# Decoder layer on one core: other instruction orders in the slots, an earlier rope table, unread TensorE products, and the last quads summed by TensorE

## The chip, the cores and the metric

The kernel runs on one core of one Trainium2 chip. The metric is the device time of one execution in microseconds; what is compared is the median over several runs. A profile shows one execution, with times from the start of its span. The engines are TensorE (PE), VectorE (DVE), ScalarE (ACT), GpSimd (POOL), and SyncE (SP), which only starts transfers.

## The reference

One decoder layer over 32 sequences of 128 tokens with 128 features, all in float32:

```python
x = layernorm(x + self_attention(x))        # 16 heads of 64, rope on 32 of the 64, causal
x = layernorm(x + cross_attention(x, ctx))  # 16 query heads of 8, 4 key/value heads, rope, key mask
x = layernorm(x + moe(x))                   # 8 experts, top 2 of sinkhorn gates (3 rounds)
# moe(x) itself returns x + expert output, so the last sum holds 2*x
# expert: (relu(x @ wg) * (x @ wp)) @ wo, 256 hidden
```

## The kernel before

**The attention phase** (attention_phase, L92 on) is a software pipeline written out by hand. There are 36 slots, 0 to 35. In slot s five stages run, each for another sequence: f (q and k projection and rope) for sequence s, v (values) for s-1, k (self attention, output projection) for s-2, a (first norm, cross attention up to its scores) for s-3, c (cross attention from its probabilities on, second norm, router logits) for s-4. A q/k projection serves two sequences at once: even slots make the queries of a pair, odd slots the keys. So slots 0 to 3 fill the pipe, slots 4 to 31 are full, and slots 32 to 35 drain it (f is off in 32, v in 33, k in 34, a in 35). The program has no loops at run time.

**The order.** Each engine executes its own list in order. The list of a slot is the function `slot` in the block of that engine: before, one branch for `s < DRAIN_SLOT` (32) and one for the rest. Between engines there are semaphores. The products of TensorE land in seven PSUM banks, and the dictionary of SlotRing says which product uses which bank; a bank is reused in program order, so a product waits until its bank's last content was taken out (drained). Names like `k.S0` are a stage and a product: `k.S` scores, `k.PT` transposed probabilities, `k.OT` head outputs, `k.Y` the output projection; `a.T`, `a.QKV`, `a.QT`, `a.KT`, `a.S` and `c.PT`, `c.OT`, `c.O`, `c.T`, `c.Y`, `c.XT`, `c.R` are the steps of cross attention and router in their order; `f.XT`, `f.Q` and `v.V` are the transposed input, the projections and the values. Each is taken out by DVE or ACT, and which of the two does it is fixed by the list in which its `copy` stands (L649 on DVE, L486 on ACT).

**Steps that the prediction speaks of.** Rope: ACT copies a projection to `raw` (L520), POOL multiplies by the sine (L401), DVE by the cosine (rope_cos, L699); the sum is made by POOL (L410), in slots 0 and 1 by DVE (L707). Softmax: DVE takes the row maximum (L687), ACT the exponential with its sum (L505), DVE the reciprocal (L692), POOL multiplies (L395). cross_rope (L757 to L764) empties bank 0 of `a.QKV`; `f.Q2` uses bank 0 too. The second norm writes `x_all` (L723), reading SBUF alone.

**The start.** SP loads a third of the projection weights, the identity, the first inputs, then sixteen small tables, the rope tables as the seventh and eighth. In slot 0 DVE calls make_constants after x_lo: it waits for all small tables, copies the rope tables to a padded tile (L667), TensorE transposes them (turn_tables, last of its list in slot 0), DVE takes them out as cosT and sinT (L669 to L671), splits the second third of the weights (w_split(1), L655) and makes masks (L673 to L679). The rope steps need cosT and sinT. POOL splits the last third (L390) ahead of its first rope step.

**Routing.** The 32 sequences are routed in two groups, of 20 and 12. The steps of group 0 are laid at marks a, b, c, d of slots 24 to 31 (MARKS); its rows are then sent to their places in DRAM by 40 indirect transfers of POOL in slots 32 to 35 (send_rows, L1591).

**The FFN phase** (ffn_phase) works through 78 blocks of 128 gathered rows, 47 and 31; block i: transpose (L1907), three products for the hidden layer (L1914 to L1916), two transposes (L1922), two products (L1929), and POOL sends the answers (L1760). The routing steps of group 1 are laid beside blocks 0 to 23 (ROUTED), then POOL sends its 24 pieces. At the end eight quads of four sequences are joined: add the two answers (L1856), add 2x (L1861), statistics (L1867, L1872), deviation and normalise on ACT (L1788, L1796), and a store. Quads 5, 6 and 7 belong to group 1 and come last.

Of the kernel before, what the change touches and what calls it, by code (L numbers as in the profile page):

```python
# [6 lines left out]
F32 = mybir.dt.float32  # L7
# [4 lines left out]
ALU = mybir.AluOpType  # L12
# [10 lines left out]
COLS = 512  # L23
# [10 lines left out]
class SlotRing:  # L34
# [5 lines left out]
    def __init__(self, sem, banks, last):  # L40
        self.orders = [list(banks), list(last)]
# [7 lines left out]
    def count(self, s, name, back=0):  # L49

        total = 0
        for slot in range(s - back + 1):
            mates = [other for other in self.orders[slot >= DRAIN_SLOT] if self.banks[other] == self.banks[name]]
# [6 lines left out]
EVEN = ("f.XT0", "f.XT1")  # L60

# [58 lines left out]
def attention_phase(nc, sem, ps, x2_all, logits, ident, mhalf, eps, scratch, x, ctx, qmask, kpad, cosq, sinq,  # L120
# [5 lines left out]
    with ExitStack() as phase:  # L126
        def sb(name, shape, dt=F32):
# [104 lines left out]
        ident_loaded = sem("ident_loaded")  # L232
        wqkv_loaded = [sem(f"wqkv_loaded{third}") for third in range(3)]
# [38 lines left out]
                 (xwo_sb[:], xwo), (rw_sb[:], rw), (rb_sb[:], rb), (cos_sb[:], cosq), (sin_sb[:], sinq),  # L272
# [95 lines left out]
        def _(pool):  # L368
# [62 lines left out]
            def slot(s, r, f, v_, k, a, c):  # L431
                p = r % 2
                if s < DRAIN_SLOT:
# [7 lines left out]
                    if on(f):  # L441
                        rope_add(s, r, 0)
                    if on(k):
                        norm_fill(k, 2)
# [1561 lines left out]
```

## Time and profile before

| | |
|---|---|
| median of 3 runs | 991.24 us (989.80 to 991.57) |
| the profiled execution, its own time | 994.09 us |
| its span | 992.3 us |
| granted TensorE clock, mean of the span | 0.92 |
| busy | PE 834.2, DVE 694.7, ACT 673.9, POOL 647.7 us |

The page of the profile gives busy time by engine and 40 slices of the span. Other views cut it into stretches, group instructions by line and shape, list who waited for whom, or list instructions in order of time. A full slot is the stretch from one `k.S` product group (L1000) to the next.

### The profile page before, as it was taken

The numbers are of one execution on the slowest core, as the hardware profiler recorded it, in microseconds if no ns is written. First come the engines' busy times: TensorE is split into PE (matmuls) and PEld (weight loads), VectorE is DVE, ScalarE is ACT, GpSimd is POOL, SyncE is SP. The second block draws the span as 40 slices with busy tenths as digits, with TensorE's granted clock in tenths as the row PEclk, the third lists the DMA queues.
The fourth block names the chain that finished last, engine by engine and source line by source line (L and its number), as shares of the span: only waits on it lengthen the run. The fifth ranks groups of instructions, "written<-read, shape, count | busy, mean of one in ns | idle before, by whom it ended". The sixth has DMA issues, their size and how long they took to land. (4 is left out here: it accounts for less than half of the span.)

```text
span 992.3 us, 22962 instructions
## 1 busy us (share of the span) xinstructions
PE 834.2 (84%) x7560; PEld 662.6 (67%) x7592; DVE 694.7 (70%) x1885; ACT 673.9 (68%) x2427; POOL 647.7 (65%) x706
## 2 busy tenths in 40 slices
PE   3689999999999999999988988897766698179990
PEld 2577787877878777788867776775543476157760
DVE  4647878888788887888888888885455466035674
ACT  3358878888788887888887787785464353035564
POOL 4477867878678786787876667677656145745551
PEclk7789999999999999999999999998885599579995
DMA  4000409900000000000000000000101511141334
GB/s 126 6 7 12 125 23 131 103 12 7 15 8 15 13 7 16 7 13 14 8 15 7 12 7 13 6 7 18 35 24 44 133 36 36 52 117 45 111 89 127
DMA packets 63506, 39.81 MB, mean 40 GB/s; under 512 B 15936, under 2 KB 60224, under 8 KB 63392
## 3 DMA queue, kind: packets, MB, share of 16 engines
q1 hardware_dynamic: 58848, 28.89, 13.4%
q0 software_dynamic: 4544, 9.45, 2.9%
q8 instruction: 65, 1.06, 0.5%
q14 instruction: 49, 0.40, 0.1%
HBM read 21.51 MB, written 16.81 MB: 39 GB/s over the span
## 5 line engine op out<-in xcount | busy, mean ns | idle before, releaser
L401 POOL TENSOR_TENSOR crossed<-raw,sinT 128x512 f32<-128x512 f32 x128 | 162.9, 1283 | 162.5 <-ACT raw L520 156.5
L505 ACT ACTIVATE prob<-ps,negmax 128x128 f32<-128x128 f32 x512 | 181.3, 383 | 81.1 <-DVE negmax L687 81.1
L395 POOL TENSOR_TENSOR prob<-prob,recip 128x512 f32<-128x512 f32 x128 | 133.0, 1048 | 12.0 <-DVE recip L692 11.8
L513 ACT ACTIVATE xprob<-ps,xmax 128x128 f32<-128x128 f32 x512 | 136.0, 416 | 7.0 <-DVE xmax L687 6.8
L1760 POOL DMA_INDIRECT answered<-ysb,goes_to x78 | 76.2, 977 | 91.8 <-DVE ysb L1851 58.9
L687 DVE TENSOR_REDUCE negmax<-ps 128x4 f32<-128x512 f32 x128 | 84.2, 679 | 43.7 <-PE ps L1000 30.9
L505 ACT ACTIVATION_READ_ACCUMULATOR prob<-ps,negmax 128x1 f32 x512 | 114.2, 223 | 0.0
L934 PE MATMUL ps<-ident,xprob 128*128 128x128 f32 x514 | 83.5, 288 | 18.8 <-ACT xprob L513 8.1
L972 PE MATMUL ps<-xT_hi,w_lo 128*128 128x256 f32 x256 | 82.6, 323 | 13.5 <-DVE xv L764 6.3
L687 DVE TENSOR_REDUCE xmax<-ps 128x4 f32<-128x512 f32 x128 | 82.2, 684 | 16.6 <-remote 9.5
L520 ACT ACTIVATE raw<-ps 128x512 f32<-128x512 f32 x128 | 80.5, 629 | 16.8 <-POOL crossed L401 10.3
L934 PEld LDWEIGHTS ps<-ident,xprob 128*128 128x128 f32 x514 | 61.6, 146 | 29.3 <-DVE xprobT L649 10.3
L410 POOL TENSOR_TENSOR kR<-kR,crossed 128x512 f32<-128x512 f32 x60 | 76.2, 1280 | 4.1 <-DVE kR L699 2.9
L934 PE MATMUL ps<-ident,prob 128*128 128x128 f32 x512 | 73.6, 278 | 6.2 <-POOL prob L395 4.7
L410 POOL TENSOR_TENSOR qR<-qR,crossed 128x512 f32<-128x512 f32 x60 | 76.1, 1280 | 1.2
L1591 POOL DMA_INDIRECT placed<-x_all,place x64 | 63.3, 988 | 18.3 <-issue 18.3
L973 PE MATMUL ps<-xT_lo,w_hi 128*128 128x256 f32 x256 | 74.1, 290 | 0.0
L974 PE MATMUL ps<-xT_hi,w_hi 128*128 128x256 f32 x256 | 74.1, 289 | 0.0
L1000 PE MATMUL ps<-kR,qR 32*128 32x128 f32 x2048 | 70.3, 285 | 0.5 <-DVE kR L707 0.4
L1019 PE MATMUL ps<-probT,v 128*64 128x128 f32 x1024 | 69.8, 279 | 0.5 <-issue 0.5
L1000 PEld LDWEIGHTS ps<-kR,qR 32*128 32x128 f32 x2048 | 63.5, 194 | 7.2 <-issue 6.2
L1845 DVE TENSOR_TENSOR h<-ps,gs 128x256 f32<-128x256 f32 x78 | 33.1, 424 | 50.0 <-ACT gs L1779 27.3
(221 smaller groups left out, 2246.3 us busy)
## 6 DMA issues: line engine op xcount, KB each, us to landing
xg<-placed SPq DMA_DIRECT2D x8, 528.0 KB, 6.6
yq<-answered SPq DMA_DIRECT2D x8, 512.0 KB
placed<-fw_hi SPq DMA_DIRECT2D x1, 3008.0 KB, 17.4
xf<-in_x SPq DMA_DIRECT2D x32, 64.0 KB, 2.9
xres<-in_x SPq DMA_DIRECT2D x32, 64.0 KB, 1.8
cx<-in_ctx SPq DMA_DIRECT2D x32, 64.0 KB, 1.8
out_y<-yo SPq DMA_DIRECT2D x8, 256.0 KB, 2.3
placed<-fw_hi SPq DMA_DIRECT2D x1, 1984.0 KB, 25.4
```

The source lines that it names most:

```text
L395: nc.gpsimd.tensor_tensor(prob[:, n], prob[:, n], recip[:, n, :, None].broadcast_to([128, 4, S]), ALU.mult).then_inc(normed, 1)
L401: nc.gpsimd.tensor_tensor(crossed[n % 2][:], raw[n % 2][:, ::-1], sinT[:, :, None, :].broadcast_to([128, 2, 2, S]), ALU.mult).then_inc(sin ...
L410: nc.gpsimd.tensor_tensor(dst, dst, crossed[n % 2][:], ALU.add).then_inc(roped, 1)
L505: last = nc.scalar.activation(prob[:, n, j, :], bank(name)[:, j * S:(j + 1) * S], ACT.Exp, bias=negmax[:, n, j:j + 1], accum_out=sums[:, n ...
L513: last = nc.scalar.activation(xprob[:, n, g, :], bank(name)[:, g * S:(g + 1) * S], ACT.Exp, bias=xmax[:, n, g:g + 1])
L520: nc.scalar.activation(raw[n % 2][:].rearrange("p a b s -> p (a b s)"), bank(f"f.Q{n}"), ACT.Copy).then_inc(raw_ready, 1)
L687: nc.vector.tensor_reduce(dst, bank(name).rearrange("p (j s) -> p j s", j=4), AX_X, ALU.max, negate=True).then_inc(done, 1)
L934: return nc.tensor.transpose(dst, src, ident[:])
L972: nc.tensor.matmul(part, w_lo[:, at:at + S], hi[:], start=True, stop=False)
L973: nc.tensor.matmul(part, w_hi[:, at:at + S], lo[:], start=False, stop=False)
L1000: last = nc.tensor.matmul(bank(f"k.S{n}")[:, g * S:(g + 1) * S], qR[pair][rows, g, ab, p, :], kR[rows, g, ab, p, :], start=False, stop=(g ...
L1760: nc.gpsimd.indirect_dma_start(answered[g], bass.IndirectOffsetOnAxis(goes_to[g][:, j:j + 1], 0), ysb[:, i, :], None, bounds_check=plan.si ...
```

## The change

What it does, part by part:

- **Full slots.** Other lists for all four engines in slots 0, 1 and 4 to 31, and another bank for most products. On DVE the copies of `c.PT1`, `c.OT`, `v.V1` and `c.XT` are new, on ACT those of `c.PT2` and `k.PT0`.
- **Slots 2 and 3** get lists of their own (FILL_SLOTS).
- **Slots 32 to 35** get other lists.
- **Slot 0.** The rope tables are loaded right after the first third of the weights and are turned right after the first input. w_split(1) moves behind the second rope step, the masks to the end of slot 1, POOL's split of the last third to the end of slot 0.
- **Unread products.** `busy(s, n)` issues n products of 128x512 in bf16 into the free bank 7 in slots 34 and 35, where nothing reads them: 27 in slot 34, 22 in slot 35, 8 behind slot 35, 3 of 128x128 in float32 at the first block of the FFN phase, 8 of 128x512 in float32 behind its last block.
- **Last quads.** For quads 6 and 7 TensorE makes the sum in PSUM: twice the identity times x, plus the identity times each of the two answers. DVE takes the statistics from PSUM. The second half of quad 7 is normalised by DVE, the first by ACT, and the shift and normalise of a quad of group 1 now stand ahead of the moments of the next.

The diff, cut to its core:

```diff
+FILL_SLOTS = (2, 3)
...
         ring = SlotRing(sem, {
...
-            "a.T": 1, "c.PT3": 2, "a.QKV": 0, "c.OT": 2, "v.V0": 1, "c.O": 2, "k.PT0": 4, "v.V1": 5, "c.T": 1, "k.PT1": 2,
-            "f.Q1": 3, "c.Y": 6, "f.Q2": 0, "f.Q3": 1, "k.PT2": 2, "k.PT3": 4, "k.OT0": 3, "a.QT": 5, "a.KT": 6, "k.OT1": 4,
+            "a.T": 1, "f.Q0": 6, "c.OT": 0, "v.V0": 1, "c.O": 0, "a.QKV": 6, "f.Q1": 5, "c.T": 1, "v.V1": 2, "k.PT0": 1,
+            "c.Y": 0, "k.PT1": 4, "f.Q2": 6, "k.PT2": 3, "k.OT0": 1, "k.PT3": 2, "f.Q3": 4, "a.QT": 3, "a.KT": 0, "k.OT1": 2,
...
             sp.dma_start(stage[0], third(wqkv, 0)).then_inc(wqkv_loaded[0], 16)
+            sp.dma_start(cos_sb[:], cosq).then_inc(rope_loaded, 16)
+            sp.dma_start(sin_sb[:], sinq).then_inc(rope_loaded, 16)
             sp.dma_start(ident[:], ident_d).then_inc(ident_loaded, 16)
...
-            pool.wait_ge(w_hi_ready, 3)
-            nc.gpsimd.tensor_tensor(third(w_lo, 2), stage[2], third(w_hi, 2).bitcast(F32), ALU.subtract).then_inc(w_lo_ready[2], 1)
             pool.wait_ge(tables_made, 1)
+            def w_split():
+                pool.wait_ge(w_hi_ready, 3)
+                nc.gpsimd.tensor_tensor(third(w_lo, 2), stage[2], third(w_hi, 2).bitcast(F32), ALU.subtract).then_inc(w_lo_ready[2], 1)
...
+            dve.wait_ge(rope_loaded, 32)
+            dve.wait_ge(pads_set, 2)
+            for i, table in enumerate((cos_sb[:, 0:ROPE // 2], sin_sb[:, ROPE // 2:ROPE])):
+                nc.vector.tensor_copy(turning[i][:, :, 0, :], table[:, None, :].broadcast_to([128, 4, ROPE // 2])).then_inc(pads_made, 1)
             w_split(0)
...
+                        if s == 0:
+                            make_tables()
...
+                        if s == 0:
+                            w_split(1)
...
+                        if s == 1:
+                            make_constants()
...
-                if isinstance(s, int) and s == 1:
-
+                if s == 2:
                     pe.wait_ge(w_loaded, 16 * len(small))
                     pe.wait_ge(masks_made, 1)
                     pe.wait_ge(const_ready, 4)
 
+                def busy(s, n):
+
+                    if s < B + 2:
+                        return
+                    for _ in range(n):
+                        nc.tensor.matmul(ps[:, 7, :], identb[:], causal[:].rearrange("p j s -> p (j s)"), start=True, stop=True)
...
             slots(pe, slot)
+            for _ in range(8):
+                nc.tensor.matmul(ps[:, 7, :], identb[:], causal[:].rearrange("p j s -> p (j s)"), start=True, stop=True)
...
+        SUMMED = {left[-2]: [5], left[-1]: [6, 7]}
         for q in left:
-            late_steps += [(name, q) for name in ("add", "twice", "stats", "moments", "deviation")]
+            if q not in SUMMED:
+                late_steps += [("add", q), ("twice", q)]
+            late_steps.append(("stats", q))
+            if q > left[0] and plan.quads[q - 1][0]:
+                late_steps += [("shift", q - 1), ("normalise", q - 1)]
+            late_steps += [("moments", q), ("deviation", q)]
...
+            nc.vector.tensor_scalar(twin[:], ident[:], 2.0, None, ALU.mult).then_inc(twin_made, 1)
...
                         x_transpose(0)
+                        for _ in range(3):
+                            nc.tensor.matmul(ps[:, DOWN, 0:128], ident[:], ident[:], start=True, stop=True)
...
+            for q in SUMMED:
+                b0 = plan.quads[q][1]
+                sums(q, twin, x2_all[:, b0:b0 + FB, 0:D], True, False)
+
+            for _ in range(8):
+                nc.tensor.matmul(ps[:, UP[0], :], ident[:], x2_all[:, 0:FB, 0:D], start=True, stop=True)
+            for q in SUMMED:
+                pe.wait_ge(yq_loaded[q % QB], 16 * (quads_before(q % QB, q) + 1))
+                sums(q, ident, yq[q % QB][:, :, 0:D], False, False)
+                sums(q, ident, yq[q % QB][:, :, D:2 * D], False, True).then_inc(quad_summed, 1)
```

How instructions move, at three places.

DVE at the start, from its first instruction to the first rope step of slot 0, before (`w_lo` is w_split, `qR<-ps,cosT` the first rope step):

```order
L655 SCALAR_TENSOR_TENSOR w_lo<-prob,w_hi 128x4x128 x2
L727 TENSOR_TENSOR xT_lo<-ps,xT_hi 128x256
L667 COPY xprob<-cos_sb 128x4x16
L667 COPY xprob<-sin_sb 128x4x16
L669 COPY cosT<-ps 128x128
L670 TENSOR_SCALAR sinT<-ps 128x128
L671 COPY sinT<-ps 128x128
L655 SCALAR_TENSOR_TENSOR w_lo<-prob,w_hi 128x4x128 x2
L673 CAST qm_all<-qm_u 128x32
...
L1406 RECIPROCAL rtemp<-rtemp 128x1
L699 TENSOR_TENSOR qR<-ps,cosT 128x512
```

and with the change:

```order
L741 COPY xprob<-cos_sb 128x4x16
L741 COPY xprob<-sin_sb 128x4x16
L732 SCALAR_TENSOR_TENSOR w_lo<-prob,w_hi 128x4x128 x2
L806 TENSOR_TENSOR xT_lo<-ps,xT_hi 128x256
L746 COPY cosT<-ps 128x128
L747 TENSOR_SCALAR sinT<-ps 128x128
L748 COPY sinT<-ps 128x128
L778 TENSOR_TENSOR qR<-ps,cosT 128x512
```

The second w_split and the masks left the way to the first rope step; w_split(1) now stands behind the second rope step, the masks behind the last one of slot 1.

DVE in slot 24, the middle of the slot, before (`la<-dif,rlog` is a routing step, `xt` and `xv` are cross_rope, `xo` is `c.O` divided):

```order
L743 TENSOR_TENSOR xo<-ps,xrec 128x128
L692 RECIPROCAL recip<-sums 128x4
L649 COPY probT<-ps 128x512
L1444 TENSOR_TENSOR la<-dif,rlog 128x160
L757 TENSOR_TENSOR xt<-ps,xcos_sb 128x160
L762 TENSOR_TENSOR xt<-ps,xsin_sb 128x20x4 x2
L764 COPY xv<-ps 128x4x8
```

and with the change:

```order
L822 TENSOR_TENSOR xo<-ps,xrec 128x128
L771 RECIPROCAL recip<-sums 128x4
L766 TENSOR_REDUCE negmax<-ps 128x4
L771 RECIPROCAL recip<-sums 128x4
L836 TENSOR_TENSOR xt<-ps,xcos_sb 128x160
L841 TENSOR_TENSOR xt<-ps,xsin_sb 128x20x4 x2
L843 COPY xv<-ps 128x4x8
L1669 TENSOR_TENSOR la<-dif,rlog 128x160
L726 COPY v<-ps 128x512
```

cross_rope now stands ahead of the routing step, and a copy of values stands where one of probabilities stood earlier.

TensorE in slot 35, before (`xprob` are the four `c.PT`, then `c.OT`, `c.O`, `c.T`, `c.Y`, `c.XT`, `c.R`):

```order
L934 MATMUL ps<-ident,xprob 128x128 x16
L1074 MATMUL ps<-xprobT,xv 32x512 x4
L934 MATMUL ps<-ident,xoT 128x128 x4
L934 MATMUL ps<-ident,xo 128x128
L1091 MATMUL ps<-xwo_sb,xonT 128x128
L934 MATMUL ps<-ident,x_all 128x128
L1099 MATMUL ps<-rw_sb,x2T 128x8
```

and the same stretch with the change, from the last `c.PT` on (`causal,identb` at L1247 and L1463 are unread products):

```order
L1070 MATMUL ps<-ident,xprob 128x128 x4
L1247 MATMUL ps<-causal,identb 128x512 x3
L1210 MATMUL ps<-xprobT,xv 32x512 x4
L1247 MATMUL ps<-causal,identb 128x512 x2
L1070 MATMUL ps<-ident,xoT 128x128 x4
...
L1227 MATMUL ps<-xwo_sb,xonT 128x128
L1247 MATMUL ps<-causal,identb 128x512 x6
L1070 MATMUL ps<-ident,x_all 128x128
...
L1235 MATMUL ps<-rw_sb,x2T 128x8
L1463 MATMUL ps<-causal,identb 128x512 x8
```

The read products are the same and keep their order; unread ones stand between them.

## Rows read from the trace of the kernel before

**Rows 1.** The page: busy time by engine, its share of the span and instructions.

```profile
PE 834.2 (84%) x7560; PEld 662.6 (67%) x7592; DVE 694.7 (70%) x1885; ACT 673.9 (68%) x2427; POOL 647.7 (65%) x706
```

**Rows 2.** Stretches of the span: length, busy time of PE, PEld, DVE, ACT, POOL, clock.

```profile
38.10:59.50 21.40, 17.19 (x165) 15.07 (x166) 8.10 (x18) 11.44 (x43) 13.84 (x12) 0.76 0.03 9
59.50:82.30 22.80, 19.66 (x187) 16.84 (x187) 13.31 (x34) 16.58 (x62) 16.30 (x18) 0.85 0.03 9
82.30:499.20 416.90, 403.31 (x4221) 328.48 (x4240) 339.64 (x853) 353.98 (x1312) 317.34 (x340) 1.00 0.18 31
499.20:681.80 182.60, 164.67 (x1704) 133.10 (x1710) 154.61 (x399) 146.00 (x545) 128.48 (x136) 1.00 0.03 9
681.80:713.50 31.70, 22.00 (x191) 15.62 (x191) 14.02 (x39) 15.90 (x62) 18.33 (x22) 0.80 0.10 31
713.50:741.00 27.50, 19.22 (x178) 14.39 (x177) 11.98 (x34) 13.29 (x54) 17.51 (x20) 0.86 0.10 31
741.00:777.40 36.40, 20.88 (x79) 12.33 (x79) 18.53 (x48) 14.06 (x39) 19.68 (x23) 0.55 0.12 36
```

**Rows 3.** Instructions in order of time, 9 to 21 us: start, length, what.

```profile
9.37 0.60 ACT L520 ACTIVATE raw<-ps 128x512 f32<-128x512 f32 x1 [2.27 <-PE ps L974]
...
13.55 0.89 DVE L667 COPY xprob<-cos_sb 128x64 f32<-128x64 f32 x1 [5.91 <-DMA eidx_sb<-in_eidx]
...
15.91 2.35 DVE L655 SCALAR_TENSOR_TENSOR w_lo<-prob,w_hi 128x512 fp32r<-128x512 f32 x2
...
20.53 0.69 DVE L699 TENSOR_TENSOR qR<-ps,cosT 128x512 f32<-128x512 f32 x1
```

**Rows 4.** Groups by line and shape in slots 13 and 14: DVE and ACT copies.

```profile
L649 DVE COPY v<-ps 128x512 f32<-128x512 f32 x2 | 1.4, 692 | 0.6 <-PE ps L986 0.6
...
L486 ACT ACTIVATE x2T<-ps 128x128 f32<-128x128 f32 x2 | 0.6, 283 | 0.0
```

**Rows 5.** Waits in 501 to 685 us: total, times, longest.

```profile
PEld ps L972 <- DVE xv L764: 7.3, 5, 2.4
```

**Rows 6.** Waits in 640 to 777 us.

```profile
DVE negmax L687 <- remote: 12.9, 2, 6.5
...
DVE xmax L687 <- remote: 9.5, 2, 4.8
```

**Rows 7.** The costliest group of TensorE in 741 to 777 us.

```profile
L934 PE MATMUL ps<-ident,xprob 128*128 128x128 f32 x28 | 7.1, 424 | 7.1 <-ACT xprob L513 7.1
```

**Rows 8.** Three bf16 products of 128x512 in a row, at 59 and 712 us.

```profile
58.72 0.81 PE L989 MATMUL ps<-causal,identb 128*128 128x512 bf16 x3
...
712.08 1.46 PE L989 MATMUL ps<-causal,identb 128*128 128x512 bf16 x3 [3.60 <-DVE logits L749]
```

**Rows 9.** The end of the attention phase and the first product of FFN blocks 2, 3, 6 and 7.

```profile
775.76 0.17 DVE L749 TENSOR_TENSOR logits<-ps,rb_sb 128x8 f32<-128x8 f32 x1 [0.39 <-PE ps L1099]
777.38 7.62 SPq L1721 DMA_DIRECT2D xg<-placed  x6
...
784.42 0.79 PE L1914 MATMUL ps<-fw_hi,x_lo 128*128 x1
787.20 0.78 PE L1914 MATMUL ps<-fw_hi,x_lo 128*128 x1
...
796.12 0.49 PE L1914 MATMUL ps<-fw_hi,x_lo 128*128 x1
797.91 0.49 PE L1914 MATMUL ps<-fw_hi,x_lo 128*128 x1
```

**Rows 10.** The last quads: DVE and ACT in order of time.

```profile
977.76 0.69 DVE L1856 TENSOR_TENSOR acc<-yq 128x512 f32<-128x512 f32 x1 [4.06 <-DMA yq<-answered]
...
979.21 0.87 DVE L1867 BATCH_NORM_STATS2 st<-acc 128x6 f32<-128x128 f32 x4
...
986.29 3.17 ACT L1796 ACTIVATE yo<-acc,nmr,rstd 128x128 f32<-128x128 f32 x8
```

**Rows 11.** Line 723, all its instructions: count, shortest, median, longest in ns.

```profile
L723 DVE TENSOR_SCALAR x_all<-y,mv,rstd x32: 337/1286/1299, 95.0 to 773.8; 128x128 f32<-128x128 f32 x32
```

More of the change, by code:

```diff
@@ L34, with __init__ @@
 class SlotRing:
-    def __init__(self, sem, banks, last):
-        self.orders = [list(banks), list(last)]
+    def __init__(self, sem, banks, first, last):
+        self.orders = [list(banks), list(first), list(last)]
         self.banks = banks
@@ L52, in count @@
         for slot in range(s - back + 1):
-            mates = [other for other in self.orders[slot >= DRAIN_SLOT] if self.banks[other] == self.banks[name]]
+            mates = [other for other in self.orders[2 if slot >= DRAIN_SLOT else 1 if slot in FILL_SLOTS else 0] if self.banks[other] == self.banks[name]]
             for other in mates if slot < s - back else mates[:mates.index(name) + 1]:
@@ L870, in slot @@
                     if on(c):
-                        copy(s, "c.PT0", xprobT[:, 0].rearrange("p j s -> p (j s)"))
+                        copy(s, "c.PT1", xprobT[:, 1].rearrange("p j s -> p (j s)"))
+                    if on(a):
+                        normalise(a, y1, mv1, rstd1, x1c[1 - p][:], rstd1_ready, x1_ready)
                     if on(k):
@@ L1206, in slot @@
                         xo_back()
+                    for stage_ in marked("pe", s, "b"):
+                        routing.pe(pe, 0, stage_)
+                    if on(a):
+                        xqkv()
+                    if on(f):
+                        qk(1)
+                    if on(c):
+                        xo_transpose()
+                    if on(v_):
+                        values(1)
+                    if on(k):
+                        prob_transpose(0)
+                    if on(c):
+                        xout()
@@ new lines, in slot @@
+                    if on(k):
+                        prob_transpose(1)
+                    if on(f):
+                        qk(2)
+                    if on(k):
+                        prob_transpose(2)
+                        pv(0)
+                    for stage_ in marked("pe", s, "c"):
+                        routing.pe(pe, 0, stage_)
+                    if on(k):
+                        prob_transpose(3)
+                    if on(f):
+                        qk(3)
+                    if on(a):
+                        xqk_transpose()
@@ new lines, in slot @@
+                    if on(k):
+                        pv(1)
+                    if on(c):
+                        x2_transpose()
+                    if on(a):
+                        xscores(0)
+                        xscores(1)
+                        xscores(2)
+                    if on(c):
+                        router()
+                    if on(a):
+                        xscores(3)
+                    for stage_ in marked("pe", s, "d"):
+                        routing.pe(pe, 0, stage_)
@@ L1215, in slot @@
                         xout()
+                        busy(s, 6)
                     if on(k):
@@ L1877, in shift, with normalise @@
                     .then_inc(nmr3_ready, 1)
-            quad_steps = {"add": add, "twice": twice, "stats": stats, "moments": moments, "shift": shift}
+            def normalise(q):
+                if q < left[-1]:
+                    return
+                dve.wait_ge(nmr3_ready, q + 1)
+                wait(dve, stored[q % QB], 16 * quads_before(q % QB, q))
+                for j in range(FB // 2, FB):
+                    nc.vector.tensor_scalar(yo[q % QB][:, j, :], joined(q, j), rstd3[q % QB][:, j:j + 1], nmr3[q % QB][:, j:j + 1],
+                                            ALU.mult, ALU.add).then_inc(yo_ready, 1)
+            quad_steps = {"normalise": normalise, "add": add, "twice": twice, "stats": stats, "moments": moments, "shift": shift}
+            nc.vector.tensor_scalar(twin[:], ident[:], 2.0, None, ALU.mult).then_inc(twin_made, 1)
             split_x(0)
@@ L1953, in _, with sums @@
                     expert_down(i - 2, owners.pop(i - 2))
+            def sums(q, weights, src, start, stop):
+                each = FB // len(SUMMED[q])
+                for n, at in enumerate(SUMMED[q]):
+                    last = nc.tensor.matmul(ps[:, at, 0:each * D], weights[:], src[:, n * each:(n + 1) * each, :], start=start, stop=stop,
+                                            skip_group_check=True)
+                return last
+            pe.wait_ge(twin_made, 1)
+            for q in SUMMED:
[7 more added lines that the diff above has]
+                sums(q, ident, yq[q % QB][:, :, D:2 * D], False, True).then_inc(quad_summed, 1)
 def _tables():
```

461 lines of the change are left out of this document (310 added, 151 removed), and 14 rows, old and new, of the table ring.

## The prediction

> **What bounds the kernel now.** I read the page first: PE is busy 84% of the span, DVE 70, ACT 68, POOL 65 [rows 1]. A share over the whole span mixes stages, so I cut the span where a slot's first k.S product starts [rows 2]. Slots 4 to 23 take 416.9 us, 20.85 each, at the full clock (1.00 is 2.4 GHz), with PE busy 403.3: TensorE's list is the bound, and only 13.6 us, 0.68 per slot, are idle. Slots 24 to 31, which carry the routing steps, take 182.6 us, 22.8 each, with PE idle 17.9. The fill and the drain are chains of short steps over all engines: slots 2 and 3 take 21.4 and 22.8 us though two and one of their stages are missing, slots 32 and 33 take 31.7 and 27.5, and slots 34 and 35 with the barrier 36.4 at a mean clock of 0.55, so nearly all at 1.2 GHz. Behind that the FFN phase is paced by its blocks [rows 9], and the end by three quads in a row [rows 10].
>
> The profiled execution took 994.09 us, 1.8 more than its span and 2.85 above the median of 991.24. I sum against 994.09 and take 2.85 off at the end. A measurement of this kernel can tell about 0.2%, 2 us, from no change.
>
> **The start.** The first rope step begins at 20.53 us, though its input is copied by 9.97 (9.37 + 0.60) [rows 3]. DVE idles 5.91 us for the last small table, then turns tables, splits weights (2.35 from 15.91) and makes masks (18.26 to 20.53, 2.3). With the change the tables come early; I set the step at 11 us, a microsecond past the copy for the two loads now ahead of the input: 9.5 us off. 2.35 come back behind the second rope step and 2.3 before slot 2, whose first product waits for the masks; POOL's split, about as long, now stands before slot 1's rope steps. Left are 2.5 to 4.9 us. I take -3, and bounds of 0 (the rope chain was the bound, not its start) and -7.
>
> **Slots 2 and 3.** TensorE is idle 4.2 and 3.1 us there and runs partly at half clock [rows 2]. New lists can win at most those 7.3. The chain scores, exponential, normalisation, transposes, output projection stays; qk(0) moves ahead of the scores, qk(1) and both value products ahead of the first transpose, so less is left for the end. I take -3, bounds +2 and -7.
>
> **Full slots, 20 of them.** Work on TensorE is unchanged; a new order can only take idle time away, at most 0.68 a slot. DVE gains one large copy net (PT1, OT, V1 for PT2 and k.PT0, 0.69 us) and XT (I take ACT's 0.28) [rows 4], so 17.0 (339.6 / 20) becomes 18.0 of 20.85; ACT falls from 17.7 to 16.7. Nothing comes to its limit. I take -0.25 a slot, -5; bounds -13.6, and +5 if each slot loses as much.
>
> **Slots 24 to 31.** Against 20.85 a slot they cost 15.8 us extra. One wait has a name: qk(2) needs the bank that cross_rope empties, and cross_rope stands behind a routing step: 7.3 us [rows 5]. Now cross_rope stands ahead of it. Late next is DVE itself: 19.3 (154.6 / 8) plus 1.0 is 20.3 busy of 22.8. I take -6, bounds -15.8 and +5.
>
> **Slots 32 and 33.** 59.2 us with TensorE idle 18.0. Four times DVE waits long before a row maximum, 22.4 us in all, and the view names no engine (remote) [rows 6]. I can't say from the list alone what it waited for, so I don't count on that. Value products now stand before the scores and fill a gap. I take -3, bounds +4 and -10.
>
> **Slots 34 and 35.** TensorE's 20.9 busy us at clock 0.55 would be 11.5 at the full one, 9.4 less; TensorE waits for others half the time (a transpose group has as much idle before it, 7.1 us, as work [rows 7]), so half of that is on the path: -4.7. The price: three bf16 products take 0.81 us at full clock and 1.46 at half [rows 8], which makes 0.22 and 0.43 each. 49 are 10.8 us at full clock; they fit in the idle time, but a product that becomes ready behind them waits for those issued. Up to six stand in one place, where the wait is long; I take +1.3 for all. The eight behind slot 35 last 1.8 us where DVE's last step ends at 775.93 and SP goes on at 777.38 [rows 9]: about +1.3 to the barrier. Net -2, bounds +3 and -6.
>
> **FFN start.** The first products of blocks 2 and 3 are 2.78 us apart, those of blocks 6 and 7 1.79 [rows 9]. If the clock is up when the phase starts, three to four blocks win 0.99 each less some waiting: -3, bounds 0 and -4. The routing of group 1 is laid by blocks, so what is won here lasts through its dispatch.
>
> **The last quads.** From the first add to the last normalise it is 977.76 to 989.46 [rows 10]. Quads 6 and 7 lose add and twice, 1.4 us each on DVE (quad 5: 1.45 from add to statistics). In their place TensorE sums; a float32 product of 512 columns has no row. Four times the 0.25 us of rows 7 (7.1 for 28) is 1.0 at mostly half clock, 0.5 at full; two per quad, and twice that if each is two passes: 1 to 2 us a quad at full clock, up to 4 at half. At full clock the sums of quad 7 end some 1.5 us before the old place of its statistics. Behind the statistics stood deviation and eight normalise pieces (3.17); now four of them go ahead, and the last four are shared by two engines: 0.9 less. I take -2.4, bounds +1 and -4.
>
> **Sum:** -3 -3 -5 -6 -3 -2 -3 -2.4 = -27.4, so 966.7 profiled and **963.8 us** as a median, -2.8%. With each term near its size, 954 to 973.
>
> **Rivals.**
> A, *the full slots win nothing*: the idle 0.68 a slot is the cost of waits that any order has, and DVE's copy eats what routing slots win. Without -5 and -6: -16.4, 974.8 us. For it speaks that PE idle is so small already.
> B, *the full slots win more*: half of all PE idle goes there (-7) and most of the routing excess (-12): another -8 to -12, about 954 us.
> C, *the unread products do not hold the clock*. Against it: in the full slots, where PE is busy 97%, it stays at 1.00; for it: slots 32 and 33 are busy 70% and still are at 0.80 and 0.86 [rows 2]. Then 49 products are 21.1 us in 15.5 us of idle time, +5.6, the eight +3, nothing is won in the drain, the FFN start and the last quads: -3 -3 -5 -6 -3 +8.6 = -11.4, 979.8 us. The Trainium skill speaks for this rival (TensorE: Matmul & The Clock Gate, A second HAM failure mode): small idle times between groups of matmuls can make the clock go back and forth. By that rule, too, it is 979.8; the clock of 0.80 at 70% busy agrees with it.
> D, *slower: DVE becomes what a slot waits for*. DVE's waits (3.9 us idle a slot) are for products and ACT, so they stay where they are; the extra 1.0 us then lengthens each of 28 slots: +28 -16.4 = +11.6, 1002.8 us. It decides from 0.59 us a slot (16.4 / 28). For it: three copies now stand before the first row maximum, and routing slots already have DVE at 85%. Against it: 18.0 of 20.85 is no more than ACT had.
> What two engines take from each other bears on D: the second norm takes 1286 ns at the median and 337 when nothing runs on POOL [rows 11], 0.95 us a slot that a better place would give back. The Trainium skill has a rule for it (SBUF — State Buffer, Who interferes with whom): VectorE and GpSimd share one port pair, and the one that comes second waits for the whole instruction; a VectorE instruction with at most one SBUF input, outside its two-port modes, is not held up. By that rule the added copies cost their 1.0 us and no more, and the traces' 0.69 for such copies agrees.
>
> **How the numbers follow.** Forecast 0.45; A 0.18; B 0.13; C 0.12; D 0.12. The range reaches over A and C and to most of B, and leaves out D and the far ends: 944 to 986. Only D gives a slower kernel; a mild form of it would land near no change: faster 0.87, same 0.02, slower 0.11.
>
> **What would show it.** First rope step near 11 us, first k.S product of slot 2 some 3 us earlier. Slots 4 to 23 at 20.6 us or below and 24 to 31 near 22, with the wait for xv gone; if DVE's idle time per slot is as before and the slot longer, D is right. Clock 1.00 from 741 us on in the stretches that were 0.55, 1.8 us between FFN blocks at once; if it stays at half with PE busy, C is right. Last statistics about 1.5 us earlier. I am wrong if a full slot grows, or if the drain takes as long as before.

## The result, and the profile after

The changed kernel takes 969.39 us (median of 5 runs, 964.84 to 972.67), the one before 990.61 in the runs beside it: ratio 0.9775, interval 0.9753 to 0.9798, so 2.25% faster. The forecast was 963.8, -27.4 us, with a range of 944 to 986. The profiled execution took 964.84 us, the lowest of the five; against the 994.09 of the profile before that is -29.25, while the medians differ by 21.2. Of the 8 us between the two, 4.55 are that the new kernel's profile lies below its median, and 3.5 that the old one's lies above. The terms below are read from that pair; a second profile of the changed kernel (E9) and those of other runs say how far to trust them.

The page of the changed kernel:

```profile
span 963.0 us, 23188 instructions
PE 850.0 (88%) x7689; PEld 657.9 (68%) x7689; DVE 710.3 (74%) x1935; ACT 654.9 (68%) x2374; POOL 648.4 (67%) x706
PEclk8799999999999999999999999999989999579999
```

The stretches that answer to [rows 2], each from a slot's first k.S product, but the last from slot 34's first transpose of xprob; it ends at the load of the next FFN rows, where SP passes the barrier (length, then busy time of PE, PEld, DVE, ACT, POOL, and the clock):

```profile
36.00:54.60 18.60, 15.46 (x167) 13.06 (x166) 7.70 (x17) 10.76 (x42) 13.25 (x12) 0.91 0.01 2
54.60:76.40 21.80, 18.88 (x190) 15.94 (x189) 15.64 (x35) 16.52 (x62) 16.97 (x18) 0.92 0.03 10
76.40:488.80 412.40, 408.44 (x4243) 324.82 (x4242) 350.07 (x894) 340.76 (x1270) 317.76 (x340) 1.00 0.18 32
488.80:673.70 184.90, 168.24 (x1710) 133.53 (x1709) 162.55 (x414) 140.93 (x532) 128.22 (x136) 0.99 0.03 9
673.70:701.30 27.60, 19.40 (x185) 13.77 (x184) 12.81 (x37) 16.61 (x64) 19.15 (x23) 0.94 0.10 33
701.30:723.50 22.20, 17.15 (x167) 13.06 (x167) 9.62 (x30) 12.84 (x52) 15.60 (x18) 0.85 0.10 32
723.50:755.40 31.90, 25.55 (x140) 12.72 (x140) 19.15 (x48) 14.99 (x43) 20.83 (x25) 1.00 0.14 45
```

The drain is compared from marks that both kernels have: slot 32's first score product, slot 34's first transpose of xprob (737.3 before, 723.5 now), and the load at the barrier. The barrier ends the attention phase, once all engines are through it, GpSimd with its sends too. The column "term" is what the prediction had.

| part | before | now | change | term |
|---|---|---|---|---|
| first k.S product of slot 2 | 38.1 | 36.0 | -2.1 | -3 |
| slots 2, 3 | 44.2 | 40.4 | -3.8 | -3 |
| slots 4 to 23 | 416.9 | 412.4 | -4.5 | -5 |
| slots 24 to 31 | 182.6 | 184.9 | **+2.3** | **-6** |
| slots 32, 33 | 55.6 | 49.7 | -5.9 | -3 |
| slots 34, 35 and barrier | 40.0 | 31.9 | **-8.1** | **-2** |
| FFN up to the last quads | 200.4 | 195.0 | -5.4 | -3 |
| last quads | 11.7 | 9.85 | -1.85 | -2.4 |

One row got longer. Slots 24 to 26 are 3.3 us shorter, slots 27 to 31 are 5.6 longer (115.2 to 120.8). Instructions in order of time at the start of slot 30, VectorE and then TensorE:

```profile
622.25 0.29 DVE L1720 TENSOR_REDUCE held<-ps 128x8 f32<-128x160 f32 x1
622.58 1.00 DVE L1722 TENSOR_SCALAR held_i<-held 128x8 int32<-128x8 f32 x1
623.61 0.17 DVE L1724 TENSOR_SCALAR padded_i<-held_i 128x8 int32<-128x8 int32 x1
623.82 0.17 DVE L1726 CAST padded<-padded_i 128x8 f32<-128x8 int32 x1
624.02 0.17 DVE L1728 TENSOR_TENSOR_SCAN ends<-unit,padded 128x8 f32<-128x8 f32 x1
624.12 1.27 DVE L726 COPY xprobT<-ps 128x512 f32<-128x512 f32 x2
...
627.91 1.29 DVE L766 TENSOR_REDUCE negmax<-ps 128x4 f32<-128x512 f32 x2 [0.92 <-PE ps L1136]
```

```profile
622.97 0.38 PE L1125 MATMUL ps<-causal,identb 128*128 128x512 bf16 x1
624.85 0.39 PE L1125 MATMUL ps<-causal,identb 128*128 128x512 bf16 x1 [1.50 <-DVE xprobT L726]
```

A routing step of five small instructions (622.25 to 624.12) stands ahead of the copies of c.PT0 and c.PT1. A causal fill is the product (`causal,identb`) that writes the mask into a bank before the scores are added. The fill of k.S1, at 622.97, does not wait. The fill of k.S0, at 624.85, needs the bank that the first of these copies empties, so TensorE sits 1.50 us, and the scores come as much later; VectorE then sits 0.92 us until they are there. The step stood ahead of the copy of c.PT0 in the kernel before too. What is new is the bank, in the dictionary of SlotRing:

```diff
-            "k.S2": 3, "c.PT0": 1, "k.S1": 5, "k.S3": 6, "k.S0": 0, ...
+            "c.PT0": 5, "k.S2": 4, "k.S3": 3, "c.PT1": 1, "c.PT2": 6, "k.S1": 2, "k.S0": 5, ...
```

Before, k.S0 had bank 0 and c.PT0 bank 1; now k.S0 follows c.PT0 in bank 5. Over 550 to 674 us, slots 27 to 31, the view of waits gives the loss a name that the kernel before did not have:

```profile
PEld ps L1125 <- DVE xprobT L726: 9.8, 5, 2.8
PE ps L1125 <- DVE xprobT L726: 8.0, 4, 2.4
```

### The profile page after: what moved, and what is told of

Its sections match the earlier page's. It is cut to its first block and busy times, and to the rows that moved or that the text cites. A ratio compares the mean times of both kernels' runs of the same rounds, so it can differ in the third digit from the quotient of the medians.

```text
span 963.0 us, 23188 instructions
## 1 busy us (share of the span) xinstructions
PE 850.0 (88%) x7689; PEld 657.9 (68%) x7689; DVE 710.3 (74%) x1935; ACT 654.9 (68%) x2374; POOL 648.4 (67%) x706
## 5 line engine op out<-in xcount | busy, mean ns | idle before, releaser
L539 ACT ACTIVATE prob<-ps,negmax 128x128 f32<-128x128 f32 x512 | 183.6, 409 | 98.5 <-DVE negmax L766 98.5
L407 POOL TENSOR_TENSOR prob<-prob,recip 128x512 f32<-128x512 f32 x128 | 131.0, 1042 | 16.8 <-DVE recip L771 16.3
L539 ACT ACTIVATION_READ_ACCUMULATOR prob<-ps,negmax 128x1 f32 x512 | 127.5, 249 | 0.0
L520 ACT ACTIVATE probT<-ps 128x512 f32<-128x512 f32 x126 | 79.1, 677 | 18.0 <-PE ps L1070 18.0
L1070 PE MATMUL ps<-ident,prob 128*128 128x128 f32 x512 | 79.5, 279 | 6.4 <-POOL prob L407 4.5
L1070 PE MATMUL ps<-ident,xprob 128*128 128x128 f32 x514 | 78.9, 277 | 6.7 <-issue 1.7
L1070 PEld LDWEIGHTS ps<-ident,xprob 128*128 128x128 f32 x514 | 58.5, 141 | 31.4 <-ACT xprob L547 20.9
L726 DVE COPY xprobT<-ps 128x512 f32<-128x512 f32 x92 | 60.2, 680 | 20.4 <-PE ps L1070 18.8
L1070 PEld LDWEIGHTS ps<-ident,prob 128*128 128x128 f32 x512 | 57.7, 142 | 22.9 <-issue 15.2
```

The lines of the kernel that those rows point to most:

```text
L407: nc.gpsimd.tensor_tensor(prob[:, n], prob[:, n], recip[:, n, :, None].broadcast_to([128, 4, S]), ALU.mult).then_inc(normed, 1)
L520: nc.scalar.activation(dst, bank(name, n), ACT.Copy, scale=scale).then_inc(ring.drained[ring.bank(name)], 1)
L539: last = nc.scalar.activation(prob[:, n, j, :], bank(name)[:, j * S:(j + 1) * S], ACT.Exp, bias=negmax[:, n, j:j + 1], accum_out=sums[:, n ...
L1070: return nc.tensor.transpose(dst, src, ident[:])
```

## The experiments

All edits but E10's are to the changed kernel. "Slots 27 to 31" is the distance of score products as above. The runs fell on several chips. E1 to E4, E9, E10 and E11 fell on two on which the kernel before takes 990.8 and 990.9 us, as it does beside the changed kernel; times are compared with that. E5 to E8 fell on one where it takes 938.4.

**E1, no unread products.** `busy()` returns at once, and the eight behind slot 35 go:

```diff
                 def busy(s, n):
-                    if s < B + 2:
-                        return
+                    return
...
-            for _ in range(8):
-                nc.tensor.matmul(ps[:, 7, :], identb[:], ...)
```

> The changed kernel without any unread product in slots 34 and 35 and without the eight behind slot 35 (41 + 8 fewer bf16 products; the rest of its lists stay). Theory 'clock': they are what keeps TensorE at 1.00 from 712 us to 821, so without them slots 34 and 35 run at half clock as before, and the stretch from the first product of slot 34 to the load of the first FFN rows grows from 31.9 us by 6 to 8, the first FFN blocks by 2 more: about 978 us as a median against 969.4. Theory 'order': the new lists of slots 34 and 35 gave those 8.1 us, and the unread products cost queueing and 1.3 us at the barrier: the stretch stays at 32 or falls to 30, 967 to 970 us.

The products that go are 49 and 8; the 41 above is a miscount. 974.36 us (974.0 to 975.34), 3 to 5 above the changed kernel (969.39, and 971.41 in E9), but only 1.2 above E3, which ran beside it and whose edit changed nothing. Slots 34, 35 with the barrier, then the first FFN blocks:

```profile
726.60:761.40 34.80, 19.79 (x83) 12.49 (x83) 19.13 (x48) 14.86 (x43) 19.12 (x23) 0.65 0.12 37
761.40:780.50 19.10, 16.78 (x81) 12.63 (x81) 10.32 (x42) 8.84 (x31) 4.65 (x5) 0.83 0.68 171
```

The clock falls to 0.65, where it is 0.86 to 1.00 in the five runs that have the products and the sends in their place (changed kernel, E2, E3, E9, E11), so the products do hold it up. But the stretch is 34.8 us, not 38 to 40: of the 8.1 us the products gave 2.9 by the first profile (31.9), and the new order 5.2. By E2 and E3, which ran beside E1, they gave 1.5 (33.2 and 33.3), by E9 0.5 (34.3), and E11 took 36.0 with them. So their gain here is no larger than what the stretch moves by itself. The next stretch, as far as the ninth block, took 17.8 us in the changed kernel (17.8 to 18.1 in these five): about one us of the FFN term is theirs. Both theories were half right.

**E2, the first routing step behind the copies.**

```diff
-                    for stage_ in marked("dve", s, "a"):
-                        routing.dve(dve, 0, stage_)
                     if on(c):
                         copy(s, "c.PT0", ...)
                         copy(s, "c.PT1", ...)
                         copy(s, "c.PT3", ...)
                     if on(a):
                         normalise(a, y1, ...)
...
+                    for stage_ in marked("dve", s, "a"):
+                        routing.dve(dve, 0, stage_)
                     if on(k):
                         scores_max(s, "k.S0", ...)
```

> The changed kernel with VectorE's first routing step of each slot moved from ahead of the copies c.PT0, c.PT1 and c.PT3 to behind them and the first norm, just ahead of the row maximum of k.S0. Theory 'place': slots 27 to 31 became longer (24.2 us each, 23.0 before the change) because three banks that the causal fills need come free one routing step later; with the copies first TensorE's waits for xprobT (18.4 us in all over the program) go, and the step falls into the 1.0 us in which VectorE waits for k.S0: 22 to 22.7 us a slot, 7 to 10 us less for the five, about 961 us. Theory 'load': VectorE's work itself, 21.0 us of 24.2 (19.5 of 23.0 before), sets these slots; what goes from the fills comes back as a wait for the row maxima: 23.8 to 24.2 a slot, 968 to 970 us.

962.52 us (960.55 to 962.87), 0.9706 of the kernel before (0.9662 to 0.975), 6.9 below the changed kernel's median. Slots 27 to 31 fall from 120.8 to 112.1:

```profile
549.40:661.50 112.10, 104.40 (x1067) 82.47 (x1070) 100.47 (x265) 86.71 (x325) 80.26 (x86) 1.00 0.03 9
```

Over these five slots both waits of L1125 for DVE's xprobT are gone, and VectorE's wait for the scores (negmax <- PE) falls from 6.4 to 0.8 us. So one edit of place gives back all 5.6 us and 3 more. Slots 24 to 31 take 176.2 us, 6.4 below the kernel before. Theory "place" holds.

**E3 and E8, less work on VectorE.** c.PT3 of slots 28 to 31 moves to ScalarE, alone (E3) and with E2's edit (E8). VectorE's side of it, the other being the same copy behind c.PT2 in ScalarE's list:

```diff
                         copy(s, "c.PT1", ...)
-                        copy(s, "c.PT3", ...)
+                        if s < 28:
+                            copy(s, "c.PT3", ...)
```

> The changed kernel with the copy c.PT3 of slots 28 to 31 on ScalarE, behind c.PT2, in place of VectorE: 0.65 us less on VectorE in each of four slots. Theory 'load': each of these slots becomes at least 0.65 us shorter, 2.6 us for slots 27 to 31 together (120.8 to 118). Theory 'place': ScalarE copies c.PT3 while VectorE is still in its routing step, but c.PT0 and c.PT1 stay behind it and their banks are needed just as early: under 1 us less for the five slots. In both about 967 to 969 us, so the trace's stretch decides, not the time.

> The changed kernel with both edits: the first routing step behind the three copies (112.0 us for slots 27 to 31, against 120.8) and c.PT3 of slots 28 to 31 copied by ScalarE (alone 122.5 against 120.8 to 122.5, nothing). If VectorE's work is what is left of the bound there (21 us busy of 22.4), taking 0.65 us a slot off it now counts: 109 to 110 us for the five, 960 us. If the slots are now set by TensorE and by the chains, 112 us and 962 as with the first edit alone.

E3: 973.12 us (967.64 to 974.27), slots 27 to 31 122.5 us, as in E1 and E9, where nothing is edited there. E8: 112.0 us for them, as E2. 2.6 us of work less on the engine that is busy 87% (105.1 of 120.8 us) changed nothing twice: theory "load" falls. It also tells that c.PT3 is not the copy that counts; whether c.PT1 adds to c.PT0 no run separates. E8's time is told with E5's.

**E11, the third routing step moved as well.** With E2's edit, E6's, and

```diff
-MARKS["dve"] |= {(28, "a"): [GATES], (28, "c"): [TOP0], (29, "a"): [TOP1], (29, "c"): [WEIGHT], (30, "a"): [ENDS],
-                 (30, "c"): [PLACE], (31, "a"): [SLOT], (31, "c"): [TABLE]}
+MARKS["dve"] |= {(28, "a"): [GATES], (28, "d"): [TOP0], (29, "a"): [TOP1], (29, "d"): [WEIGHT], (30, "a"): [ENDS],
+                 (30, "d"): [PLACE], (31, "a"): [SLOT], (31, "d"): [TABLE]}
```

> The changed kernel with three edits: the first routing step behind the three copies, slots 2 and 3 on the lists of the full slots (alone one us better), and the third routing step of slots 28 to 31 (TOP0, WEIGHT, PLACE, TABLE) moved from ahead of the copy v.V1 to behind the second rope step. If the third step too holds up TensorE (pv waits for v and probT), slots 27 to 31 fall from 112.0 to 108 to 110 us; if not they stay at 112. In all 10 to 13 us below the changed kernel on the same chip.

A miss: 971.42 us (970.16 to 973.82), and slots 27 to 31 take 124.8, 12.7 more than in E2. Slot 28, VectorE at the new place and the product that waits:

```profile
584.85 1.27 DVE L1697 TENSOR_TENSOR cand<-cand,eidx_sb 128x160 f32<-128x160 f32 x1
...
587.45 1.27 DVE L1704 SCALAR_TENSOR_TENSOR dif<-one,la 128x160 f32<-128x160 f32 x1
588.64 0.17 DVE L1705 COPY x_all<-low 128x20 f32<-128x20 f32 x1
588.73 0.68 DVE L812 TENSOR_TENSOR xkT<-ps,gsel 128x512 fp32r<-128x512 f32 x1
```

```profile
589.50 1.62 PE L1194 MATMUL ps<-xkT,xqT 128*128 128x512 f32 x3 [4.34 <-issue]
```

The step's seven instructions stand ahead of cross_k, whose xkT the scores of the cross attention need: TensorE sits 4.34 us. The view calls that "issue"; the time at which xkT is ready tells it. The third step stood well where it was.

**E10, the wait for xv alone.** It is what the term of -6 for slots 24 to 31 was built on. The kernel before, one edit:

```diff
-                    for stage_ in marked("dve", s, "c"):
-                        routing.dve(dve, 0, stage_)
                     if on(a):
                         cross_rope(s, a, p)
+                    for stage_ in marked("dve", s, "c"):
+                        routing.dve(dve, 0, stage_)
```

> The kernel before the change with a single edit: in slots 24 to 31 VectorE's cross_rope stands ahead of the third routing step, not behind it. It tries the failed step alone. Theory of the prediction: the wait of qk(2) for xv (7.3 us) goes and with it 5 to 7 us of slots 24 to 31 (182.6 before the change). Theory 'place': it goes too, but what sat behind the routing step, the copies of the next banks, now comes later, and 0 to 3 us are won. Time: 4 to 7 us, or 0 to 3 us, below the kernel before.

987.76 us, ratio 0.9956 (0.9933 to 0.998) to 990.9: 3.1 us faster, by the interval 2 to 7. The wait for xv is gone, and slots 24 to 31 go from 182.6 to 179.1, all of it in slots 27 to 31 (115.2 to 112.0):

```profile
499.10:678.20 179.10, 163.92 (x1699) 132.66 (x1706) 156.01 (x399) 145.40 (x544) 128.03 (x135) 1.00 0.03 9
```

Of a wait of 7.3 us half was time. This lies between the two theories' bounds. Nothing is edited behind slot 31, so E10 is also a second profile of the old drain and FFN phase.

**E6, slots 2 and 3 on the full slots' lists.** `FILL_SLOTS = ()` for `(2, 3)`.

> The changed kernel with no lists of their own for slots 2 and 3: they take those of the full slots. The change won 3.8 us from slot 2's first k.S product to slot 4's (44.2 to 40.4). Theory 'the lists of slots 2 and 3 gave it': the stretch goes back to 43 to 45 us, time +3. Theory 'the new full-slot lists and the early tables would have given it too': 40 to 42 us, time within 1 us of the changed kernel.

Slot 2 starts at 34.1 us, 1.9 sooner, and slots 2 and 3 take 39.0 us, inside the 38.1 to 41.2 of the runs with lists of their own. So these lists give nothing: slot 4 starts at 73.1 (74.0 in E11, which is without them too), and at 74.0 to 77.7 with them. The 3.8 us come from what else changed; no run takes that apart.

**E7, the last quads as before.** `SUMMED = {}`, all eight last normalise pieces on ScalarE, no unread products there.

> The changed kernel with the last three quads summed and normalised as before the change: add and twice on VectorE, all eight last normalise pieces on ScalarE, none of the eight unread products ahead of the sums. Theory of the prediction: 2.4 us of the end are lost again; from the first add of quad 5 to the end of the last normalise 11.5 to 12.3 us instead of 9.85. Rival: the half shared normalise alone gave it (0.9) and the sums on TensorE nothing, because quad 7's rows come late: then the last statistics start at most 0.5 us later than now (955.67 less 950.35 is 5.3 us behind the first add) and the end 0.9 us later.

From the first add to the last normalise 11.61 us (911.07 to 922.68), against 9.85: 1.8 us. The last statistics stand 6.7 us behind the first add, 5.3 in the changed kernel:

```profile
917.76 0.87 DVE L2111 BATCH_NORM_STATS2 st<-acc 128x6 f32<-128x128 f32 x4
```

The sums on TensorE, with the eight products ahead of them, give 1.4 of it, and 0.4 are left for the shared normalise; the rival falls.

**E4, GpSimd's sends spread.** In slots 32 and 33 the four row sends ahead of the first normalisation go one by one behind the normalisations and the cross addition, then six go in a row. Two fewer a slot are made there, and slot 35 makes 8 in place of 4:

```diff
+                elif s < B + 2:
...
+                    if on(k):
+                        norm_fill(k, 0)
+                    send_rows(s, 0, 1)
...
+                    send_rows(s, 4, 10)
...
-PIECES = 12
+SENT = (0, 10, 20, 32)
```

> The changed kernel with GpSimd's row sends of slots 32 and 33 taken from ahead of the first normalisation (4 in a row) and put one by one behind the normalisations, then six in a row (10 a slot instead of 12; slot 35 sends 8 instead of 4). Theory 'sends': bursts of indirect sends hold up what the other engines see of TensorE's semaphores; without the burst of four the two long waits ahead of a row maximum (5.6 and 5.0 us, named remote) go, and slots 32 and 33 with the start of 34 fall from 49.8 us to 41 to 44, less up to 3 us that slot 35 gives back before the barrier: 962 to 966 us. Theory 'not the sends': the waits stay within 1 us of that length and the time at 968 to 971.

976.1 us (973.28 to 978.81), 5 to 7 above the changed kernel. Slots 32 and 33 fall to 46.5 us, slots 34 and 35 with the barrier grow to 44.8. The long row-maximum waits went, and others came, each beside a row of sends: VectorE before a copy of xprobT, 3.74 us to 727.88 and 3.38 to 732.21. That asked for a run without sends.

**E5 and E12, no sends before the end.** The same kernel twice:

```diff
-                for n in range(PIECES * (s - DRAIN_SLOT) + first, PIECES * (s - DRAIN_SLOT) + last):
+                for n in range(2 * plan.size[0] if (s, last) == (B + 3, PIECES) else 0):
```

> The changed kernel with all 40 of GpSimd's row sends of group 0 behind the last step of slot 35, none in slots 32 to 35. The barrier then comes some 50 us late (40 sends at 1.28), so only the stretches up to it say something. Theory 'sends hold others up': no long wait named remote on VectorE is left; slots 32 and 33 to the first product of slot 34 take 40 to 44 us (49.7 in the changed kernel, 51.9 to 54.7 in the runs without another edit there, 46.5 with the burst ahead of the normalisation gone), and slots 34 and 35 end 2 to 4 us sooner after that. Theory 'not the sends': 48 us or more with waits of 3 to 5 us as before.

> The kernel with all 40 row sends behind slot 35 once more, since its first run fell where the kernel before takes 938 us and where no run showed long remote waits, with sends or without. It says something if the kernel before takes about 990 us this time. Theory 'sends hold TensorE up there': no remote wait above 1 us up to the barrier, slots 32 and 33 in 37 to 41 us as in that first run (49.7 and 52.3 in the changed kernel's two runs there), about 10 us or more less. Theory 'something else of that place': 47 us or more, with waits of 3 to 6 us ahead of a row maximum or the logits.

E5 fell on the chip on which the kernel before took 938.4 us (935.25 to 940.53), and none of the four traces from there has a wait named remote. The view gives that name to a wait for which it finds no releaser on the core. E12 fell where the kernel before took 993.3, in one execution. The two took 974.5 and 1005.93 us, one execution each; the barrier waits for the 40 sends, so these times say nothing of the edit. With no sends in the drain the two chips agree: slots 32 and 33 take 37.6 us in both runs, and E12 has no remote wait up to the barrier. VectorE at slot 32's first row maximum, changed kernel and E12:

```profile
679.45 0.69 DVE L766 TENSOR_REDUCE negmax<-ps 128x4 f32<-128x512 f32 x1 [5.04 <-remote]
```

```profile
675.96 0.69 DVE L766 TENSOR_REDUCE negmax<-ps 128x4 f32<-128x512 f32 x1 [1.43 <-PE ps L1136]
```

What ran on GpSimd meanwhile, in the changed kernel:

```profile
674.38 1.21 POOL L1816 DMA_INDIRECT placed<-x_all,place  x1 [0.36 <-issue]
675.89 0.97 POOL L1816 DMA_INDIRECT placed<-x_all,place  x1 [0.30 <-issue]
677.17 0.97 POOL L1816 DMA_INDIRECT placed<-x_all,place  x1 [0.31 <-issue]
678.44 0.97 POOL L1816 DMA_INDIRECT placed<-x_all,place  x1 [0.30 <-issue]
681.98 1.04 POOL L407 TENSOR_TENSOR prob<-prob,recip 128x512 f32<-128x512 f32 x1 [2.57 <-DVE recip L771]
```

The scores are over at 676.4 by the record, the burst at 679.4, and VectorE starts at 679.45. Theory "sends" holds for the drain where the kernel before takes 990 us.

Times on the chip at 938 us: E6 924.68, E7 927.49, E8 **914.53** us (913.91 to 914.97; ratio 0.9754, 0.9731 to 0.9777). The changed kernel was not run there; from E7 less its 1.8 us I estimate 925.7, 1.4% below the kernel before. E6, which differs from it only by lists that give nothing, agrees.

**E9, the changed kernel again.**

> The changed kernel itself once more, with nothing edited, because the kernel before took 938.4 us in the last four runs and 990.8 in those ahead of them, and no long wait named remote stood in the last four traces. If this depends on the chip, the changed kernel takes 924 to 928 us where the one before takes 938 (ratio 0.986 to 0.989, a smaller gain than 0.9775), or 965 to 973 where it takes 990; the stretches up to slot 32 agree with the first profile within 2 us in both.

971.41 us (969.65 to 978.35) where the kernel before took 990.9; ratio 0.9811 (0.9782 to 0.9839). Its profile has 38.2, 412.0, 186.5, 52.3 and 34.3 us for the five parts from slot 2 to the barrier, where the table has 40.4, 412.4, 184.9, 49.7 and 31.9. The terms of slots 4 to 31 are good to 2 us. For the drain and the FFN phase there are more profiles, of runs with nothing edited behind slot 31 (E1: the unread products alone):

| run | slots 32, 33 | slots 34, 35 and barrier | barrier to the last block's first product |
|---|---|---|---|
| before | 55.6 | 40.0 | 188.1 |
| E10, the old lists | 55.7 | 40.1 | 185.9 |
| changed kernel | 49.7 | 31.9 | 182.8 |
| E9 | 52.3 | 34.3 | 183.4 |
| E3 | 51.9 | 33.3 | 182.9 |
| E2 | 54.7 | 33.2 | 184.6 |
| E11 | 53.3 | 36.0 | 184.5 |
| E1, no unread products | 53.7 | 34.8 | 186.1 |

So the drain gained 6 to 14 us and the FFN phase 1 to 5, and the first profile, from which the terms are read, was the luckiest of them in every column.

## Why the prediction was right, and which steps failed

**Start**, -3: -2.1, and the first rope step began at 10.04 us (said: 11). Of the 10.5 us by which that step moved, most is used up before slot 2, as the text had reckoned. **Slots 2 and 3**, -3: size right, cause not. The lists of their own give nothing (E6).

**Full slots**, -5: -4.5, 20.62 us a slot. It lies between rival A (nothing) and rival B (-7). PE idle fell from 13.6 to 4.0 us, while PE's modelled busy time rose by 5.1: only half of that idle time was time. DVE's busy time rose from 339.6 to 350.1, and no slot up to 26 grew, so rival D did not come about there. The 0.95 us a slot that a better place was to give back were not there: the second norm takes 1293 to 1321 ns in every slot before 32 with the change too. The reading behind it was too simple. Of its four short instances (337 to 346 ns before) three run beside an indirect send of GpSimd and only one beside nothing; the long ones stand beside GpSimd's multiplies.

**Slots 24 to 31**, -6: the step that failed. It read "Now cross_rope stands ahead of it. Late next is DVE itself". The first half was right: the wait for xv went. Alone that gives 3.5 of its 7.3 us (E10). The second half failed: it looked for the next limit in busy time, and never asked what the new banks had put behind a routing step. They had put the fill of k.S0 there, by giving k.S0 the bank of c.PT0; that cost 5.6 us net in slots 27 to 31, and 8.7 by what E2 wins back. VectorE's load was not it (E3, E8). With E2's edit the eight slots are 6.4 us shorter than before, so the size of -6 was there to be had.

**Slots 32 and 33**, -3: -5.9, and -3.3 by E9 (-0.9 to -5.9 over the table). The remote waits, which the sum left out, are the sends of rows. They cost 12 us in these two slots (49.7 to 37.6), and more in the other profiles. Of this 1.5 to 3.6 stay where there are no remote waits (39.1 to 41.2 with the sends in E6 to E8, 37.6 without); that this is the normalisation which queues behind four sends on GpSimd is likely and was not tested by itself.

**Slots 34 and 35**, -2: -8.1, -5.7 by E9 (-4 to -8 over the table). Mis-sized. Only clock and queueing were priced, and the new lists at nothing; E1 shows the lists at about 5 and the products at 3 at most, where the text had -4.7 +1.3 +1.3, -2 net. **Rival C** is wrong: the clock was 1.00 from 723.5 us on with the products (0.86 at the least, in E11) and 0.65 without. The Trainium skill's rule that spoke for it (TensorE: Matmul & The Clock Gate, A second HAM failure mode) fits the run without them and slots 32 and 33 (0.94 and 0.85), not the filled stretch.

**FFN**, -3: -5.4. As far as the ninth block 2.7, as said (20.5 to 17.8 us behind the barrier; the first products of blocks 2 and 3 are 1.8 us apart). But E10, with the old drain, needs 18.9 us for this, so only 1.1 of it is sure. 1.2 more are in the stop behind block 28, of which the last section tells, and some 1.5 are spread thinly over all other blocks; no run here looked for their cause.

**Last quads**, -2.4: -1.85; statistics 1.4 us earlier relative to the first add (said: 1.5).

So the sum of -27.4 came near the -29.25 of the profiles by luck: one term was 8.3 us too good and three, the two of the drain and the FFN phase, were together 11.4 too small. Those three are the terms that the first profile flattered. In medians the change gave 21.2 us, 19.5 beside E9. The forecast of 963.8 was 5.6 us too low, less than the 8.3 of the failed term.

## What to carry to other kernels

When an order changes, look at what stands behind each long step at its new place, not only at the wait that goes: ask for every copy which bank it frees and who needs that bank first. When banks change, ask it again: a step that did no harm ahead of a copy does harm once a bank that is needed at once hangs on that copy. A routing step that costs little just ahead of the row maxima (E2) or ahead of a copy of values stops TensorE for 4 us ahead of cross_k (E11). The length of a wait is not its price: 7.3 us of waiting for xv gave 3.5 when removed (E10), and the fills' 8.0 us on TensorE gave 8.7 (E2). Before two profiles are compared term by term, know from a second run how much a stretch moves by itself. The fastest version is E2's edit (E8 with it is as good): 0.971 of the kernel before.

## What was new about the hardware

The largest effect of all was in no term. On some chips GpSimd's indirect sends hold up what other engines see of TensorE; on another they do not, with the same instructions in the same 0.97 us. The record numbers the chips: 15, 13 and 4 are those where the kernel before takes 990.8 to 993.3 us and the traces have remote waits, 9 is the one where it takes 938.4 and they have none. For the drain E12 shows that the sends are the cause. In the FFN phase no run moved them; there it is their place in time that speaks for it. GpSimd sends 24 pieces in a row there (812.1 to 842.4 us). Waits in 815 to 860 us, changed kernel:

```profile
DVE ysb L2091 <- remote: 17.9, 3, 9.7
DVE h L2085 <- issue: 13.8, 3, 8.2
ACT gs L2019 <- remote: 12.8, 2, 8.1
ACT x_hi L2014 <- remote: 12.6, 2, 8.7
```

The stretch around it there, and one around the same 24 sends (802.5 to 832.8) in E7 on chip 9:

```profile
815.00:858.00 43.00, 14.21 (x56) 10.02 (x56) 5.90 (x17) 5.73 (x18) 27.67 (x29) 0.60 0.32 93
```

```profile
805.00:818.70 13.70, 13.36 (x76) 10.52 (x77) 7.50 (x26) 7.06 (x24) 10.66 (x11) 1.00 0.17 56
818.70:898.90 80.20, 74.56 (x409) 57.62 (x407) 51.49 (x190) 43.49 (x142) 59.73 (x62) 0.98 0.39 121
```

TensorE is busy 14.2 of 43 us in the one and 93% or more in the other, and from the barrier to the last block's first product it is 182.8 us against 153.7. E12, which has its 40 sends elsewhere, still has this stop: 186.0 against 155.5 in E5, the same kernel. These 30.5 us are nearly all of the 31.4 between the two runs. For the changed kernel the 29.1 us and the 8.5 to 10.6 in slots 32 and 33 (49.7 against 39.1 to 41.2) are most of the estimated 44 between the chips; for the kernel before it is 52, and no trace of it was taken on chip 9. By the Trainium skill (SBUF — State Buffer, Who interferes with whom) the only contention at the ports of SBUF is for the pair that VectorE and GpSimd share; TensorE and ScalarE have no part in it. By that rule the ports would hold up neither of them here, and the waits on the slower chips need another cause. What in the chips differs, and by what path a send holds up TensorE's signals, no run here shows.
